# A two-layer gated cross-attention kernel: seven batches' gate logits in two PSUM operations, statistics behind sums, more unread products, gathers before splits

## The reference

```python
x = x + tanh(g_xattn[0]) * attention(layernorm(x), ctx, ctx)      # one head, 120 keys
x = x + tanh(g_ffn[0])   * moe(layernorm(x))                      # 12 experts, 8 of them real, top 2
x = x + tanh(g_xattn[1]) * attention16(layernorm(x), ctx, ctx)    # 16 heads
x = x + tanh(g_ffn[1])   * linear_fp8(layernorm(x))

def moe(x):
    logits = x @ gate_w.T + expert_bias
    topk_logits, topk_idx = top_k(logits, 2)
    w = softmax(topk_logits)              # expert e: silu(x @ w1[e].T) @ w2[e].T
    return sum(w_e * expert_e(x)) + w_zero * x
```

## Time and profile before

| | us |
|---|---|
| median of three runs | 371.13 |
| lowest and highest | 368.69, 371.86 |
| the profiled execution | 367.93 |
| its span, first to last instruction | 365.9 |
| TensorE busy | 338.1 |
| VectorE busy | 253.4 |
| ScalarE busy | 232.6 |
| GpSimd busy | 161.5 |

### The profile page before, as it was taken

How to read it: one execution, slowest core, us unless ns; L and a number is a source line. 1 busy time by engine, 2 the same in 40 slices (tenths; PEclk the granted TensorE clock), 3 DMA queues, 4 the chain that set the end, 5 groups by cost and what they waited for, 6 DMA issues and landing times.

```text
span 365.9 us, 8956 instructions
## 1 busy us (share of the span) xinstructions
PE 338.1 (92%) x2890; PEld 267.0 (73%) x2891; DVE 253.4 (69%) x690; ACT 232.6 (64%) x471; POOL 161.5 (44%) x211
## 2 busy tenths in 40 slices
PE   4999969888999999999999998879999999999995
PEld 2768846557899999999999973656666666666774
DVE  1479998925665655654545567878888988777696
ACT  1489958136566666665666533576678678665586
POOL 7088996199655555556556344311132132101000
PEclk9999998859999999999999999999999999999998
DMA  6999963021222222232233115112011000000005
GB/s 181 323 403 423 426 240 115 2 58 31 87 74 79 79 73 72 72 81 77 72 78 80 43 59 184 61 59 60 3 60 59 2 2 2 3 2 3 0 30 201
DMA packets 15338, 36.21 MB, mean 99 GB/s; under 512 B 3526, under 2 KB 6748, under 8 KB 13772
## 3 DMA queue, kind: packets, MB, share of 16 engines
q1 hardware_dynamic: 10508, 24.66, 18.4%
q0 software_dynamic: 3936, 10.48, 10.2%
q10 hardware_dynamic: 864, 0.66, 0.5%
HBM read 22.28 MB, written 13.52 MB: 98 GB/s over the span
## 4 chain that ended last, share of the span: by engine, by line
PE 76%; DVE 10%; ACT 5%; DMA 3%; POOL 2%; issue 2%; SPq 0%; DVEq 0%; ACTq 0%
PE two L1999 15%; PE two L1984 15%; PE two L2141 5%; PE two L2018 5%; PE two L2171 4%; PE two L2206 4%; PE two L2127 4%; PE two L2107 3%; PE two L2009 2%; PE two L2198 2%; DMA x_sb<-in_x 2%; DVE stat L1109 1%; PE two L1866 1%; PE two L2187 1%; DVE x_sb L1191 1%
## 5 line engine op out<-in xcount | busy, mean ns | idle before, releaser
L1398 DVE SCALAR_TENSOR_TENSOR gate<-th,two 128x512 f32<-128x512 f32 x39 | 26.8, 688 | 58.0 <-ACT th L869 32.6
L613 POOL DMA_INDIRECT y_d<-y_sb,goal_i x39 | 38.5, 987 | 48.6 <-ACT y_sb L879 48.3
L607 POOL DMA_INDIRECT xg<-xn_d,slot_i x39 | 37.9, 973 | 21.3 <-DVE slot_i L1343 10.4
L1984 PE MATMUL two<-wh,gh 128*128 x156 | 44.1, 283 | 0.2 <-issue 0.2
L636 POOL TENSOR_TENSOR rstd<-var,half 128x2 f32<-128x2 f32 x14 | 9.9, 706 | 76.9 <-DVE var L1463 76.9
L1984 PE MATMUL two<-wh,gl 128*128 x156 | 43.8, 281 | 0.0
L1984 PE MATMUL two<-wl,gh 128*128 x156 | 43.8, 281 | 0.0
L858 ACT ACTIVATE xq<-xg 128x256 f32<-128x256 f32 x39 | 23.5, 603 | 30.8 <-DMA xg<-xn_d,slot_i 30.2
L869 ACT ACTIVATE th<-two 128x512 f32<-128x512 f32 x39 | 23.3, 596 | 27.3 <-PE two L1999 17.4
L573 POOL TENSOR_TENSOR wl<-wl,wh 128x512 fp32r<-128x512 f32 x32 | 40.2, 1278 | 0.1
L1496 DVE TENSOR_REDUCE nm<-two 128x8 f32<-128x960 f32 x32 | 36.1, 1152 | 4.5 <-PE two L2127 4.1
(11 more groups left out here) (307 smaller groups left out, 857.6 us busy)
## 6 DMA issues: line engine op xcount, KB each, us to landing
wl<-in_wmoe SPq DMA_DIRECT2D x8, 1024.0 KB, 12.1
y_d<-wh SPq DMA_DIRECT2D x4, 1024.0 KB
yg<-y_d SPq DMA_DIRECT2D x7, 512.0 KB, 3.6
xn_d<-x_sb SPq DMA_DIRECT2D x8, 258.0 KB, 5.9
x_sb<-in_x SPq DMA_DIRECT2D x8, 256.0 KB, 6.0
out_x<-of SPq DMA_DIRECT2D x8, 256.0 KB, 2.0
xg<-xn_d,slot_i POOLq DMA_INDIRECT x39
y_d<-y_sb,goal_i POOLq DMA_INDIRECT x39
```

The costliest lines, as they stand in the source:

```text
L607: pool.indirect_dma_start(xg[:, n % 2, :], None, xn_d, bass.IndirectOffsetOnAxis(ap=slot_i[:, n:n + 1], axis=0)).then_inc(gathered[n % 2], 16)
L613: pool.indirect_dma_start(y_d, bass.IndirectOffsetOnAxis(ap=goal_i[:, n:n + 1], axis=0), y_sb[:, n % 2, :], None).then_inc(y_stored[n % 2] ...
L1398: dve.scalar_tensor_tensor(gate[:, k, :], th[:], 1.0, bank[2 + k][:], ALU.add, ALU.mult).then_inc(gate_ok, 1)
L1984: ins = pe.matmul(bank[6 + k][:, 0:D], (gl if part == 2 else gh)[:, k, a], (wl if part == 1 else wh)[:, bass.ds(e + (C * FF + c * D), D)], ...
```

## The change

- `add_x1` writes the sum of gate columns straight into `logits` (PSUM bank 4), not back into `xgate`. `logits_of(lo, hi)` works on a range of batches in two operations on PSUM: times `rstd`, plus the bias read from SBUF. It is called for batches 0 to 6 and then for batch 7, both behind the last `stats1`. The product `gate_bias`, its semaphore and the count `logit_kept` go.
- In VectorE's list `add_x1(6)` stands before `stats1(5)`, `add_x1(7)` before `stats1(6)`, and `copy_v0(6)` before `stats1(4)` and `add_x1(5)`.
- GpSimd does `low(23)` before it waits for the slots, issues four gathers at once, then two lows, a gather, a low, a gather, a low. The last four lows (28 to 31) move to VectorE, between the maximum of the last layer's weights and the next reduction.
- `busy` before the slot products grows from 9 to 16, the one behind them from 5 to 8, and the 3 before the first block become 4 ahead of `whole(1, 1, 4)` and 4 behind it.
- x of blocks 2 and 3 is turned before the h of blocks 1 and 2, not behind it.

```diff
@@ gpsimd
             low(19)
             root1(7)
-            lows(20, 23)
+            lows(20, 24)
             pool.wait_ge(slots_kept, 1)
...
-            gather(0)
-            gather(1)
-            low(23)
-            gather(2)
-            low(24)
-            gather(3)
-            lows(25, 27)
+            for n in range(4):
+                gather(n)
+            lows(24, 26)
             gather(4)
+            low(26)
+            gather(5)
             low(27)
-            gather(5)
-            lows(28, CHUNKS)
             pool.wait_ge(goals_kept, 1)
@@ vector
                 for u in range(U):
-                    dve.scalar_tensor_tensor(xgate[:, b, u, :], at[:, u, D:VP], rsum[:, u:u + 1], xgate[:, b, u, :], ALU.mult,
-                                             ALU.add)
+                    dve.scalar_tensor_tensor(logits[:, U * b + u, :], at[:, u, D:VP], rsum[:, u:u + 1], xgate[:, b, u, :],
+                                             ALU.mult, ALU.add)
...
-            def logits_of(b):
-
-                if b == 0:
-                    dve.wait_ge(gbias_done, 1)
-                dve.wait_ge(rstd1_ok, root_of(b, ROOTS1))
-                for u in range(U):
-                    ins = dve.scalar_tensor_tensor(logits[:, 2 * b + u, :], xgate[:, b, u, :], x_rstd(2 * b + u), gate_bias_at,
-                                                   ALU.mult, ALU.add)
-                ins.then_inc(logit_kept, 1)
...
+            def logits_of(lo, hi):
+
+                dve.wait_ge(gate_in, 32)
+                dve.wait_ge(rstd1_ok, root_of(hi - 1, ROOTS1))
+                t, n = slice(U * lo, U * hi), U * (hi - lo)
+                then(dve.tensor_tensor(logits[:, t, :], logits[:, t, :], wide(x3[:, t, D], E_ALL), ALU.mult))
+                then(dve.tensor_tensor(logits[:, t, :], logits[:, t, :], over(gbias_sb[:, 0:E_ALL], n), ALU.add))
...
             stats1(2)
-            logits_of(0)
             add_x1(3)
             max0_of(5)
             copy_v0(5)
             stats1(3)
-            logits_of(1)
             add_x1(4)
             max0_of(6)
+            copy_v0(6)
             stats1(4)
-            logits_of(2)
             add_x1(5)
-            copy_v0(6)
             max0_of(7)
             copy_v0(7)
+            add_x1(6)
             stats1(5)
-            logits_of(3)
-            add_x1(6)
-            logits_of(4)
+            add_x1(7)
             stats1(6)
-            add_x1(7)
-            logits_of(5)
             stats1(7)
-            logits_of(6)
-            logits_of(7)
+            logits_of(0, B - 1)
+            logits_of(B - 1, B)
...
             dve.tensor_reduce(red[:, 1:2], wf_sb[:], AX, ALU.max, apply_absolute_value=True).then_inc(red_ok, 1)
+            def low(n):
+
+                dve.wait_ge(split_h, n + 1)
+                c = cols(n, CHUNK)
+                own.mark(dve.tensor_tensor(wl[:, c], wl[:, c].bitcast(F32), wh[:, c], ALU.subtract))
+
+            for n in range(POOL_LOWS, CHUNKS):
+                low(n)
             dve.wait_ge(red_done, 1)
@@ tensor
-            busy(bank[5], 9)
+            busy(bank[5], 16)
...
-            busy(bank[5], 5)
+            busy(bank[5], 8)
             pe.wait_ge(blocks_kept, 1)
             e0, e1 = experts(0), experts(1)
+            busy(bank[5], 4)
             whole(1, 1, 4)
-            busy(bank[5], 3)
+            busy(bank[5], 4)
...
-                    pe.wait_ge(split_l, PER_EXPERT * (2 * i + k + 1))
+                    pe.wait_ge(split_l, min(PER_EXPERT * (2 * i + k + 1), POOL_LOWS))
...
-                rows_last = x and not y and (i, k) in ((-1, 0), (-1, 1))
-                if x and not rows_last:
+                if x:
                     wait_x(xi, xk)
...
-                if rows_last:
-                    wait_x(xi, xk)
-                    for c in range(C):
-                        x_part(xk, c)
```

More of the change, by code:

```diff
@@ L318, in build @@
         (xT_done, xT_copied, spread_ok, scores_done, max_done, exp_done, probT_done, probT_copied, pv_done, x1_done,
-         logit_kept, gbias_done, gsum_done, gate_ok0, wvT_done, wvT_kept, wvg_done, vg_ok, var0_ok, rstd0_ok, var1_ok, rstd1_ok) = sems(
+         gsum_done, gate_ok0, wvT_done, wvT_kept, wvg_done, vg_ok, var0_ok, rstd0_ok, var1_ok, rstd1_ok) = sems(
             "xT_done xT_copied spread_ok scores_done max_done exp_done probT_done probT_copied pv_done x1_done "
-            "logit_kept gbias_done gsum_done gate_ok0 wvT_done wvT_kept wvg_done vg_ok var0_ok rstd0_ok var1_ok rstd1_ok")
+            "gsum_done gate_ok0 wvT_done wvT_kept wvg_done vg_ok var0_ok rstd0_ok var1_ok rstd1_ok")
         xn_stored = sem("xn_stored")
@@ L459, in build @@
         PER_EXPERT = WE // CHUNK
+        POOL_LOWS = CHUNKS - PER_EXPERT
         KEYS = [(0, 0), (1, 0), (2, 0), (0, 1), (1, 1), (2, 1)]
@@ L467, in build @@
         marked = bank[4][:, BY_TILE:2 * BY_TILE].rearrange("p (t e) -> p t e", e=E_ALL)
-        gate_bias_at = bank[4][:, 2 * BY_TILE:2 * BY_TILE + E_ALL]
         @block.sync
@@ L1274, in _ @@
             stats1(3)
-            logits_of(1)
             add_x1(4)
             max0_of(6)
+            copy_v0(6)
             stats1(4)
-            logits_of(2)
             add_x1(5)
-            copy_v0(6)
             max0_of(7)
             copy_v0(7)
+            add_x1(6)
             stats1(5)
-            logits_of(3)
-            add_x1(6)
-            logits_of(4)
+            add_x1(7)
             stats1(6)
-            add_x1(7)
-            logits_of(5)
             stats1(7)
-            logits_of(6)
-            logits_of(7)
+            logits_of(0, B - 1)
+            logits_of(B - 1, B)
             dve.memset(pairs[:, TILES, :], 0.0)
-            dve.wait_ge(logit_kept, B)
             highest(0, logits)
@@ L1802, in values_gate @@
                 ins.then_inc(wvg_done, 1)
[L1804 to L1808, removed]
             def values0(b):
@@ L1893, in _ @@
             values0(0)
-            gate_bias()
             scores0(1)
```

## The result

| | before | after |
|---|---|---|
| median (lowest and highest), us | 369.01 (366.38 to 371.86) | 365.67 (363.53 to 369.19) |
| ratio, 95% interval | | 0.9884, 0.9847 to 0.9921 |
| the profiled execution, us | 367.93 | 365.97 |
| its span, us | 365.9 | 364.1 |
| mean granted clock over the span | 0.979 | 0.988 |

The change makes the kernel faster by 1.2%, 0.8 to 1.5; the ratio is worked out from fast executions alone, which leaves out the 369.19, so it is not the ratio of the two medians (0.991). The number of the forecast was near (3.2 us; the medians differ by 3.3), but its likeliest class, within 1%, was not: the interval lies beyond 1% for the most part. With its three runs the kernel before was at 371.13; with more runs its medians lie between 368.5 and 369.6.

What follows compares the result with a forecast made beforehand. TensorE, busy 338.1 of 365.9 us, was taken as the bound, with gains where it waits or runs slowly. 2.7 us up to block 4 plus 0.5 at block 6 made 3.2, off 371.13: 367.9 us, range 365.4 to 370.6.

Steps and rivals of the forecast that it cites:

- 1: First attention: logits in fewer operations and VectorE's new order gain 0.1 us, the wait moving to GpSimd's low.
- 2: Before the slots: sixteen unread products for nine fill TensorE's 1.73 us wait and keep the clock, gaining 0.15 us.
- 3: x of block 0, behind the queue of eight: 0.2 us earlier, no gain of its own.
- 4: First h runs at full clock, gaining 1.2 us.
- 5: x of blocks 2 and 3 ahead of h removes stalls at blocks 2 and 4, gaining 1.3 us.
- 6: Four lows leave GpSimd's list ahead of gather(6), so x of block 6 comes earlier, gaining 0.5 us.
- rival B: Clock falls at about 63 while TensorE waits for the rank product; slots 0.9 us later, 368.8 us; chance 0.2.
- 7: Four lows on VectorE before a reduction: 0.68 us each, covered by its idle time, gain 0.
- C: Clock falls in the register loads before block 0; 1.4 us of the gain goes, 369.3 us; chance 0.12.
- E: Block 0 set by something that stays and stalls reappear at block 4; 0.5 us left, 370.6 us; chance 0.05.
- F: Both long queues run wholly at half clock, making the kernel 1.6 us slower, 372.7 us; chance 0.08.
- D: VectorE's subtractions and GpSimd's gathers exclude each other; `xl_of(0)` 0.9 us late, 368.8 us; chance 0.1.

Runs made afterwards that it cites:

- e1: The changed kernel again, no edit; 366.23 us against 368.54 for the kernel before, ratio 0.9902.
- e3: The changed kernel with unread products as before (9 before the slots, 5 behind, 3 before the first block); 365.39 us against 368.54, ratio 0.9903.
- e4: The changed kernel with gathers, lows and rows of blocks 2 and 3 in the old order; 368.6 us against 368.54 for the kernel before, ratio 0.9996.
- e7: The changed kernel with GpSimd's last root ahead of low(19); 365.62 us against 369.14 for the kernel before, ratio 0.9913.
- e15: The changed kernel with low(24) also ahead of GpSimd's wait for the slots; 368.05 us against 369.16 for the kernel before, ratio 0.9984.
- e2: The changed kernel with the attention part undone (logits per batch, VectorE's old order); 365.71 us against 368.54 for the kernel before, ratio 0.9911.
- e6: The kernel before with only gathers first and four lows on VectorE; 367.75 us against 369.14, ratio 0.9967.
- e8: The changed kernel with 17 unread products instead of 8 before the rank product; 365.05 us against 369.14 for the kernel before, ratio 0.9897.
- e9: The kernel before with only the rows of blocks 2 and 3 turned ahead of h; 367.95 us against 369.59, ratio 0.9956.
- e5: The kernel before with the order alone: gathers first, four lows on VectorE, rows of blocks 2 and 3 first; 366.0 us against 369.14, ratio 0.9945.
- e11: The changed kernel with GpSimd's last root ahead of low(19) and 13 unread products before the rank product; 364.77 us against 369.59 before, ratio 0.9868.
- e12: e11 with one low, not two, ahead of gather(4) and the last four unread products behind the first x; 364.63 us against 369.59 before, ratio 0.987.
- e13: e11 with GpSimd doing only lows 19 to 21 before the slots, the others between gathers; 363.7 us against 369.16 before, ratio 0.9837.
- e14: e13 with 12 products before the rank product and the last four unread products between the rows of blocks 0 and 1; 363.13 us, ratio 0.9833.
- e10: e8 with one low ahead of gather(4), not two; 364.4 us against 369.59 for the kernel before, ratio 0.9877.

## Why the prediction came out as it did

Against the kernel before, in the profiled executions and net of the start:

| step | forecast | measured | from |
|---|---|---|---|
| 1 logits, attention | 0.1 | -0.1 | rsum to top |
| 2 sixteen for nine | 0.15 | -1.0 | top to slots |
| 3, 4, 5 first x, first h, rows | 2.45 | 2.6 | slots to x4 |
| 6 lows before gather(6) | 0.5 | 0.5 | x4 to x6 |
| up to block 8 | 3.2 | 2.2 | rsum to x8, 0.2 between x6 and x8 with it |

**1, right.** The wait moved to GpSimd's low(19), as the item said.

**2, wrong in sign, and this is the step that failed.** The item gave the chance 0.2 to the clock's fall at 63 (rival B), and it came in after, e1, e3 and e4, at 62 to 63 (and in e7 and e15, whose wait is longer still). The argument against it, that the clock had held after 0.5 to 1 us of idle time, was no argument for an idle time of 2.4, and the prediction had worked out "some 2.5" itself. The trace of before had a nearer case: the last attend waited 2.12 us, and the clock fell right behind it, which the prediction's account of the slow stretch (70 to 81) leaves out. TensorE alone in windows of the kernel before (busy, granted clock, DMA share, GB/s):

```profile
53.00:54.00 1.00, 1.00 (x4) 0.68 0.67 252
54.00:55.00 1.00, 1.00 (x3) 0.50 0.00 0
```

That slow stretch, 53 to 57, is also why the eight unread products "ended just on" the rank product: with the clock held and the same attention part (e2, e6) they end 0.94 us before it. What the fall costs the slots was near in size, 0.9 forecast in B against 1.28 (after less e8; against the kernel before, whose slots were themselves 0.27 above e8's, it shows as 1.0), but its working was not: the sixteen hardly ran at half clock (4.22 us against 4.03 in e8); the six products in front of them did (2.89 against 1.53). With nine products behind (e3) this delay disappears in the wait for `onerow`; with sixteen there is no wait left to take it. The queue used up the slack that the clock's fall needed. Nor do the seven more products bring anything by themselves: where the clock held up to the slots, top to slots is 12.95 and 12.97 with nine (e9, e6) and 12.96 and 12.94 with sixteen (e2, e8).

**3, mis-sized.** The longer queue behind the slots delays the first h by 0.5 (6.82 against 6.31 to 6.35 in e3, e5, e6 and e9), where nothing was charged. I had compared with the kernel before at half clock (6.63), not with short queues at their best. The prediction's own sign, a first h later than 78, came in: it starts at 78.07, though this execution reached its `rsum` 0.95 earlier than the one before.

**4, right, but not free.** 1.49 us for six against 2.65 in e3 is 1.2. Less the 0.5 of item 3, 0.65 is left at x of block 2 (8.31 behind the slots against e3's 8.97) and 0.5 at x4 (12.61 against 13.08). With item 2 the queues as a whole cost 0.8 up to block 8 in the traces, and the timing of e3 shows no difference.

**5 and 6, right,** and they carry the gain: e4 without them has none, and e5 with them alone has 3.1 us by the medians, 2.0 by the ratio. The forecast had gather(4) 9.16 behind the slots and x4 12.76; measured are 9.19 and 12.61, and the 0.35 us that it charged for a wait for gather(4) did not come: TensorE's own work set x4. What it had not said is that by the traces the two hang together (the timing does not show it): what rows-first wins at block 4 is lost at block 6, unless the four lows leave GpSimd's list.

**7, right.** 0.63 each, 0.68 taken; they ended at 76.24, before `xl_of(0)` at 77.32. C, E and F did not come. D had no price in the change itself, but its mechanism, with a low part of GpSimd's for the gather, did next to it: at `pairs` (e7, e11, e12, e15) and at the four lows (e13, e14).

**The chances.** The size of 3.2 us was near, and half a microsecond from the bound at which a gain counts as one; 0.33 for faster put more weight on the side of the bound than a scatter of 3 us in three runs bears. The reference was also the median of three high runs. The timed gain (medians 2.3 us apart in e1 and 3.3 in the first comparison, by the ratios 3.6 and 4.3) is for the most part above the trace's 2.2 up to block 8.

In the profiled execution of after the clock fell once more at 239, at the start of the second layer, where the earlier trace rows show it full: from x8 to the end is 266.2 us, before 264.8. From TensorE's wait of 0.42 us for `pT` to its wait of 0.77 us for `nm`, both in the second layer, it takes 87.75 us (239.26 to 327.01) and before 86.48 (242.24 to 328.72), so 1.3 us are the fall's. The clock fell there in e1, e3, e8 and e9 as well, between 239 and 246 us, and not in e2, e4 to e7 and e10 to e15. TensorE's waits just ahead of it, 1.22 and 0.42 us for `pT`, are the same to 0.02 us where the clock held (before, e2, e4, e5, e6, e10, e15), so they alone don't decide it; what does was not tried. On this the prediction had no sentence.

The mean granted clock of every timed execution is on record, and it accounts for part of what the medians show above the trace. In e1 the seven executions of the change at 0.988 or 0.989, the profiled one among them, took 366.1 to 367.7 us, the five at 0.993 to 0.998 took 363.9 to 365.2. An estimate from the trace of after: without the fall at 239 its 0.988 would be 0.993. So the profiled execution is one of the slower ones of its kernel. Not all of the end is explained by this: e5 and e6, without a fall at 239, take 266.4 and 266.8 us from x8 to the end, and why stays open.

## What to carry to other kernels

A queue of unread products that fills a wait to the brim keeps the clock, but it spends the slack in which a late start upstream would have disappeared: fill the first wait (here the one before the rank product) and leave slack in the second. Here that is read from the traces (e3, e8); the timings of e1, e3 and e8 lie too close to tell. Where two engines take turns on a chain, look for what the idle one does in the meantime: an operation that nobody waits for, moved by one place, took 1.1 us from the chain (e7) and the whole gain (e15). Order edits whose gains lie at successive blocks are to be priced together, at the block where the last of them frees something; here the traces say so, and the medians do not. Before a clock's fall is called unlikely, look for every place in the trace where it fell, and at the wait ahead of each.

## What the runs showed of the hardware

- A VectorE operation of two SBUF operands and a GpSimd subtraction that runs at the same time do not overlap. `pairs`, 128x128, took 0.29 us alone and 1.37, 1.41, 1.40 and 1.36 us where the fifth low part was just beginning (e7, e11, e12, e15). Four subtractions of VectorE took 2.48 to 2.52 us without one of GpSimd's beside them and 4.11 us (e13, e14) with one of 1.29 to 1.30 us inside. VectorE's operations with one operand in PSUM, 0.36 to 0.37 us, ran beside GpSimd's low parts at their usual time.
- The Trainium skill ("SBUF — State Buffer", the part on the ports) says that whichever of such two operations starts first has the shared ports for its whole instruction, and the other is blocked. That one is held up by the other agrees with the traces: in e7 the low part starts at 59.97 and ends at 61.21, and `pairs`, begun at 59.99, ends at 61.36, about half of its own length behind it. That the first to start wins does not agree with every trace as recorded. In e13 VectorE's first subtraction begins 0.40 us before low(22), which runs from 71.35 to 72.64 at its usual length, and ends 0.56 behind it:

```profile
70.95 2.25 DVE L1354 TENSOR_TENSOR wl<-wl,wh 128x512 fp32r<-128x512 f32 x1
```

e14 repeats it (70.88, 2.25 us, the low part from 71.27). In all six cases GpSimd ran at its usual length and VectorE was the one held up. Whether a recorded start is the moment at which an engine takes the ports, no run shows.
- GpSimd's gather(2), issued while VectorE's four subtractions ran, took 0.94 us in after, e1, e3 and e7, where it began 1.78 to 1.80 us behind their start, and 1.44 to 1.49 in e2, e5, e6, e8, e10, e11, e12 and e15, where it began 1.81 to 1.87 behind it. VectorE's four took 2.51 to 2.52 in the first set and 2.48 to 2.49 in the second. (In e13 and e14, where a low part stood before it, the gather took 1.24.) That is how it would look if the gather takes its turn just ahead of the fourth subtraction in the one set and waits for it in the other (the fourth begins at about 3 x 0.62 = 1.87); no run moved the gather on purpose, so this is argued and not shown.
- The granted clock fell to 1.2 GHz at 62 to 63 us in every trace in which TensorE had been idle for 2.37 to 3.44 us before the rank product (after, e1, e3, e4, e7, e15), and held where that wait was 1.39 or 1.40 (e11, e12), 0.94 (e2, e6), 0.52 (e14) or 0.24 to 0.34 us (e8, e9, e10, e13). e8, which differs from the change only by nine products in that wait, is the direct test. The length of a wait alone doesn't decide it: the 2.12 or 2.13 us before the last attend were followed by a fall in before, e5 and e9 and not in e2 and e6; the 1.70 or 1.73 us before the slot products by one in e5 and before and not in e6 and e9.
